# Last attention: the block turn moved ahead of the reciprocals on VectorE

## What is computed

```python
q = ln_lat @ Wq
kv = jnp.concatenate([xn, ln_lat], axis=1) @ Wkv
k, v = jnp.split(kv, 2, axis=-1)
weight = jnp.einsum('bhld,bhnd->bhln', q * scale, k * scale)
weight = jnp.where(full_mask[:, None, None, :], weight, neg)
weight = jax.nn.softmax(weight, axis=-1)
out = jnp.einsum('bhln,bhnd->bhld', weight, v)
return out @ Wout
```

## Time and profile before

| | |
|---|---|
| time, median of 3 runs | 2944.42 us (2942.79 to 2949.28) |
| the profiled execution, its own time | 2945.35 us |
| its span | 2943.6 us |
| PE busy | 2481.0 us, 84% of the span |
| DVE busy | 1828.4 us, 62% |
| ACT busy | 1170.7 us, 40% |
| POOL busy | 755.3 us, 26% |
| mean granted TensorE clock, share of full | 0.92 |

### The profile page before, as it was taken

The page is one execution under the profiler, slowest core; times in us unless marked ns, Lnnn a source line. Parts: engine busy times, 40 slices in busy tenths (PEclk is TensorE's granted clock), DMA queues, the critical chain, the costliest instruction groups (busy, mean ns, idle before and its releaser), DMA issues. The chain is left out here.

```text
span 2943.6 us, 35609 instructions
## 1 busy us (share of the span) xinstructions
PE 2481.0 (84%) x12608; PEld 1335.9 (45%) x12608; DVE 1828.4 (62%) x4072; ACT 1170.7 (40%) x2095; POOL 755.3 (26%) x462
## 2 busy tenths in 40 slices
PE   6888972865888699889899979989988989997996
PEld 2333331323555344545554635554454545463554
DVE  5667745246867474477767357748437875835774
ACT  1433430212323153265544146635325653514662
POOL 1002352520000042043323023414203432402441
PEclk8999985875878799999999999999999999999998
DMA  7411006974200200244320124430023442012442
GB/s 226 136 37 21 11 15 206 316 249 150 87 8 3 106 1 1 87 108 119 97 79 8 73 61 118 116 111 11 8 88 100 116 108 79 1 52 71 110 125 73
DMA packets 112959, 257.06 MB, mean 87 GB/s; under 512 B 36198, under 2 KB 56294, under 8 KB 106762
## 3 DMA queue, kind: packets, MB, share of 16 engines
q1 hardware_dynamic: 93978, 220.26, 24.8%
q10 hardware_dynamic: 12656, 25.97, 3.6%
q0 software_dynamic: 6144, 8.48, 1.0%
HBM read 119.81 MB, written 29.69 MB: 51 GB/s over the span
## 5 line engine op out<-in xcount | busy, mean ns | idle before, releaser
L858 POOL TENSOR_SCALAR pbuf<-pbuf,recip 128x1024 f32<-128x1024 f32 x128 | 364.5, 2848 | 946.0 <-DVE recip L762 946.0
L807 ACT ACTIVATE pbuf<-ps,least 128x1024 f32<-128x1024 f32 x256 | 284.3, 1113 | 295.3 <-DVE least L755 219.5
L755 DVE CUSTOM_DVE_ANT_0 ps<-ps,mask 128x1024 f32<-128x1024 f32 x256 | 307.9, 1244 | 140.2 <-PE ps L687 139.2
L584 POOL TENSOR_SCALAR pbuf<-pbuf,recip 128x512 f32<-128x512 f32 x128 | 200.2, 1576 | 459.7 <-DVE recip L505 459.7
L687 PE MATMUL ps<-kH,qT 64*128 64x512 f32 x1024 | 267.4, 642 | 49.8 <-ACT pbuf L807 47.0
L712 PE MATMUL ps<-work,vh 128*64 128x256 f32 x2048 | 251.9, 390 | 0.0
L555 ACT ACTIVATE pbuf<-ps,least 128x512 f32<-128x512 f32 x256 | 172.7, 686 | 155.6 <-DVE least L495 155.6
L769 DVE STREAM_TRANSPOSE pbuf<-pbuf 128x2048 f32<-128x2048 f32 (+1 forms) x128 | 226.3, 1768 | 0.0
L1554 ACT ACTIVATE early<-ps 128x1536 f32<-128x1536 f32 x86 | 123.9, 1441 | 200.9 <-PE ps L1369 191.7
L1632 DVE TENSOR_REDUCE mh<-ps 128x3 f32<-128x1536 f32 x86 | 150.0, 1744 | 63.8 <-PE ps L1358 61.2
L712 PEld LDWEIGHTS ps<-work,vh 128*64 128x64 f32 x2048 | 138.3, 138 | 95.2 <-issue 36.6
(11 more groups left out here) (371 smaller groups left out, 4054.7 us busy)
## 6 DMA issues: line engine op xcount, KB each, us to landing
work<-pbuf SPq DMA_DIRECT2D x784, 96.0 KB, 2.5
work<-pbuf ACTq DMA_DIRECT2D x240, 96.0 KB, 2.9
early<-in_L_wgu SPq DMA_DIRECT2D x22, 768.0 KB
expert_rows<-zero_rows SPq DMA_DIRECT2D x16, 1024.0 KB, 11.5
yg<-expert_rows SPq DMA_DIRECT2D x16, 1024.0 KB, 6.0
early<-in_L_wd SPq DMA_DIRECT2D x22, 384.0 KB
arena<-in_L_wo SPq DMA_DIRECT2D x8, 1024.0 KB, 8.8
arena<-in_L_wff SPq DMA_DIRECT2D x4, 2048.0 KB, 9.3
```

Of the source, the lines that this page charges most:

```text
L584: nc.gpsimd.tensor_scalar(x, x, recip[:, n % 8:n % 8 + 1], None, mult).then_inc(probs_ready[1], 1)
L755: nc.vector.tensor_tensor_reduce(out=x, in0=x, in1=mask, scale=1.0, scalar=FMAX, op0=add, op1=ALU.min, accum_out=least[:, n % 8:n % 8 + 1])\
L807: nc.scalar.activation(to, x, ACT.Exp, bias=least[:, n % 8:n % 8 + 1], scale=-1.0, accum_out=sums[:, n % 8:n % 8 + 1]).then_inc(taken, 1)
L858: nc.gpsimd.tensor_scalar(unit(n), unit(n), recip[:, n % 8:n % 8 + 1], None, mult).then_inc(pool_divided, 1)
```

## The change

In VectorE's iteration for pair p, `turn(p)` goes to directly behind the two searches of pair p + 1, ahead of the even slot's copy, and both reciprocals of pair p + 1 go behind that copy. No instruction is added or removed, and the other engines' streams stay as they are.

```diff
             if p + 1 < N:
                 find(2 * p + 2)
                 find(2 * p + 3)
-                invert(2 * p + 2)
+            turn(p)
             keep_jobs(2 * p)
             if p + 1 < N:
+                invert(2 * p + 2)
                 invert(2 * p + 3)
-            turn(p)
             keep_jobs(2 * p + 1)
```

## The result

| | before | changed |
|---|---|---|
| time, median | 2946.12 us (4 runs, 2942.79 to 2949.28) | 2978.82 us (4 runs, 2969.00 to 2991.99) |
| ratio, 95% interval | | 1.0107 (1.0078 to 1.0136) |
| the profiled execution, span | 2943.6 us | 2974.5 us |
| forecast, range | | 2981 us, 2960 to 2998 |

A forecast was written before the change was run, and what follows sets the result against it. TensorE, busy 84% of the span, was taken as the bound. Terms 32.6 + 7.6 + 13.8 - 2.3 - 21.8 + 7 = 36.9 us on 2945.35 gave 2982, median 2981 us; range 2960 to 2998.

The forecast's parts named there:

- Mechanism and sign: In the last attention, the new order cuts a loop of waits but makes copies late for TensorE; slower, chance 0.93.
- The loop through turn and transfers: Last attention: keys' copy, products, scores, search, exponentials, short turn, twelve transfers, exponential, copy again; one round takes 26.85 us.
- Mid-stage waits: Six groups a stage: new TensorE waits of 0.79 at position 2 and 0.57 at position 1; old waits go.
- S + 7.37: Position 2: when TensorE may go on, from score product start S; before S + 6.58, so new wait 0.79.
- S + 6.28: Position 1: when TensorE may start the values product, from score product start S; its place S + 5.71, wait 0.57.
- The new waits: Positions 1 and 2 of six groups a stage: TensorE waits for late copies, 32.6 us in four stages.
- The old ones: TensorE's earlier waits for keys (12.7) and mid-stage exponentials (7.7), plus seams, all taken off: 21.8 us.
- Start-up: First group of each stage: slot 1's copy 2.1 us later, 1.9 later in all, 7.6 us over four stages.
- Last group: Stages one to three: slots 57, 59, 61 cost 1.6, about 1.0, 2.0 more, 13.8 us; stage four returns 2.3.
- The clock: Low TensorE clock after seven long waits at slots 1 and 61: 1.0 each, 7 us; bounds 0 and 10.2.
- Heavier: Mid-stage: late reciprocals reach TensorE, 10 us more, 2991 us; with full blocks on VectorE 2997 us; chance 0.15.
- Faster: Loop cut, copies not late, needing a long turn under 1.45 us or searches 0.8 sooner: 2920 us; chance 0.04.

## Why the prediction was right

**Mechanism and sign: right.** The loop through turn and transfers was cut, TensorE's waits for exponentials in mid-stage went, and new or longer waits for copies came at the places named: positions 1 and 2, slot 1, slots 57, 59 and 61. The run with copy and turn swapped shows both that the copy's place behind the turn is the cause and that the late reciprocals are not. One statement was wrong: that cutting the loop can return about 20 us and no more, as TensorE runs back to back elsewhere. At the stages' ends it does not (in the kernel before it waited 41.6 us in the starts and 23.6 in the last parts), and the swapped kernel gained 43.4 us in the stages.

**Mid-stage waits: right to 0.1 us each.** S + 7.37 and S + 6.28 were worked out, 7.29 and 6.22 measured. VectorE began the turn at the start of its accumulator's read (both at 1345.28), not behind it as the sum had it, which is 0.13 sooner; TensorE went on 0.70 behind the copy's start, not 0.64, which takes back about half. The new waits, put at 32.6 us, were 24 x (0.71 + 0.51) = 29.3. The old ones, put at 21.8 with 20.4 of it in the wait rows, were 22.8 by the middles of the kernel in which none is left (635.6 - 612.8). With one late exponential of 0.33 that makes +6.8 for a forecast of +10.8. This is the term with the largest error among the waits.

**Start-up: right, somewhat long.** Slot 1's wait went from 1.28 to 3.14 in stage one and grew by 7.1 in the four stages (2.1 each forecast). The waits at pairs 4 and 5 did not only move along but shrank by 1.8 in all. So the starts waited 5.2 more for a forecast of 7.6, and with 3.7 of busy time for 4 of clock they cost 8.9 for 11.6. That the clock's part agrees is luck, as stage two alone carries it. That pair 4's scores would pass from an exponential to the copy of keys was right as well (2.77, ended by L3018).

**Last group: waits long, total short.** Slots 57, 59 and 61 were forecast at 1.6, 1.0 and 2.0 more than before; they wait 3.96 for 3.24, 2.49 for 1.66 and 2.51 for 0.61, so 0.7, 0.8 and 1.9. Slot 57's forecast was twice too high because of the search: a background step had held it up before (it began 2.49 us behind its score product), and now it came 2.03 behind, sooner instead of the 0.3 later that I had counted. Stage four gave 2.0 back, for 2.3 forecast. The last parts waited 8.4 more for a forecast of 11.5, but cost 16.5 for 11.5 and 3 of clock.

**The clock: the mis-sized term.** I took 7 us for seven new waits, 3 of them for slot 61. It cost up to 11.9, and 8.2 of that in the last parts. The step that failed is the count: it left out the waits that were already there and grew (slots 57 and 59). Before, stage one had these rows at the two:

```profile
1443.12 2.95 PE L712 MATMUL ps<-work,vh 128*64 128x256 f32 x16
...
1452.10 2.05 PE L3002 MATMUL ps<-arena 128*128 128x128 f32 x16 [1.66 <-DVE cnT L2814]
```

The values product behind slot 57 took 2.95 before and 3.04 in the changed kernel; up to the next wait, TensorE's busy time there grew by only 0.8 in three stages. But the products behind slot 59's wait of 2.49 took 3.37, 3.26 and 3.68, where after 1.66 they took 2.05: 4.2. Slot 61, for which I had counted 3, cost 1.7, in stage two alone, and the same stage paid another 1.7 behind the wait between the two. Since the clock was short by 5 and the waits with their seams long by 9.5 (29.9 for 20.4), the sum came out near the time; this is partly luck.

**The rivals.** Heavier: background steps behind the reciprocals do get slow beside GpSimd (L111 took 0.85 behind a reciprocal, where 0.17 stood before), but the searches have room for it, and the middle of stage one shows one wait of 0.33 and no more. Full blocks, as the Trainium skill's page "SBUF — State Buffer", section "Who interferes with whom", has them, were not seen: the step lost under a third of the 2.85 us that GpSimd's division took, and the division ran on for 1.71 us behind it. Faster: that rival named its own condition, under 1.45 us ahead of the copy. The run with half a turn met it at position 2, and the wait there vanished.

## What to carry to other kernels

On an engine that serves others in program order, the price of moving something forward is paid by what it passes. List everything the moved instruction now stands ahead of, and for each the moment at which another engine wants it; here a 2.24 us turn passed a 0.6 us copy that had 1.45 us to spare. If the short, awaited instruction goes first, the long one starts 0.6 us later: the same idea with two lines swapped is 1.3% faster than the kernel before instead of 1.1% slower. And price what stands ahead at nothing below the slack, and above it by the excess. Where the awaited engine is TensorE and the waits are long (here 2.3 to 4.0 us), count those that only grew too, and give the clock behind them a range: at slot 59 it cost between nothing and 1.6 us for a wait of 2.49.

## What the runs showed of the hardware

- VectorE's next instruction can start together with the read of the search's accumulator (both at 1345.28), so a search costs its successor 1.19 us, not 1.33.
- Nearly equal waits of TensorE got unlike clocks. Behind 2.77 us the scores of pair 4 took 1.99 in stage one, behind 2.49 us the values took 3.37, and behind 3.96 us the first transposes took 0.66, with the products behind them at 3.04 for 1.95. In the changed kernel TensorE was busy for 212.9, 220.6 and 215.5 us in stages one to three, for the same work: single stages differ by 8 us by the clock's chance. The same wait in the same place shows it best: behind 2.77 us, pair 4's scores took 1.99, 2.79, 1.99 and 2.76 us in stages one to four. The changed kernel's four runs, which spread over 23 us, go the same way: the shortest had a mean granted clock of 0.922, the longest one of 0.912.
- A very small VectorE step (128 x 4) took 0.85 us instead of 0.17 when it ran behind a reciprocal that had released GpSimd; the steps after it were short again while GpSimd was still at work. It ended 1.13 us behind the start of the division and 1.71 ahead of its end. In the kernel before, two other such steps (L106 and L113) took 0.90 and 0.92 beside a division and ended at the same point of it. In the run with one reciprocal ahead of the turn the step (L111) began 2.47 us into a division, took 0.40 and ended 0.02 behind it.
